# Moving three layer norms and six key transfers in the prologue of an attention and mixture-of-experts kernel

## The reference

```python
def _layernorm(x, axis=-1, eps=1e-05):
    m = jnp.mean(x, axis=axis, keepdims=True)
    v = jnp.var(x, axis=axis, keepdims=True)
    return (x - m) / jnp.sqrt(v + eps)
...
        Q = (query @ Wq.T + bq).reshape(B, Sq, H, dk).transpose(0, 2, 1, 3)
        K = (key @ Wk.T + bk).reshape(B, Sk, H, dk).transpose(0, 2, 1, 3)
        V = (value @ Wv.T + bv).reshape(B, Sk, H, dk).transpose(0, 2, 1, 3)
        scores = jnp.einsum('bhqd,bhkd->bhqk', Q, K) / jnp.sqrt(jnp.float32(dk))
        causal = jnp.tril(jnp.ones((Sq, Sk), dtype=bool))
        scores = jnp.where(causal, scores, -jnp.inf)
        attn = jax.nn.softmax(scores, axis=-1)
        out = jnp.einsum('bhqk,bhkd->bhqd', attn, V)
        out = out.transpose(0, 2, 1, 3).reshape(B, Sq, D)
        return out @ Wo.T + bo
...
    x = x + _L0_xattn_ref(_layernorm(x, axis=-1), ctx_1024, ctx_1024, ...)
    x = x + _L0_ffn_ref(_layernorm(x, axis=-1), ...)
```

## Time and profile before

| quantity | value |
|---|---|
| median of 3 timed runs | 502.96 us |
| lowest, highest | 500.89, 503.76 us |
| the profiled execution, its own time | 502.17 us |
| its span from first to last instruction | 500.3 us |
| granted TensorE clock, mean | 0.982 |
| busy: TensorE, DVE, ACT, POOL | 92%, 62%, 42%, 39% of the span |
| first projection of the loop over batches | 45.76 us after the start |

### The profile page before, as it was taken

The page is one execution under the profiler, slowest core; times in us unless marked ns, Lnnn a source line. Parts: engine busy times, 40 slices in busy tenths (PEclk is TensorE's granted clock), DMA queues, the critical chain, the costliest instruction groups (busy, mean ns, idle before and its releaser), DMA issues.

```text
span 500.3 us, 10299 instructions
## 1 busy us (share of the span) xinstructions
PE 458.4 (92%) x3154; PEld 318.9 (64%) x3155; DVE 308.2 (62%) x651; ACT 210.1 (42%) x420; POOL 193.1 (39%) x204
## 2 busy tenths in 40 slices
PE   7868999999999999988699799999999999999993
PEld 6644344654447443554256366599999999999852
DVE  4984757477563757656674796855554554555436
ACT  2254666517572566517862352523322322322210
POOL 4123545114541336201512002126666766665420
PEclk9998999999999999999979899999999999999998
DMA  8593322422124121400298900014344344444279
GB/s 263 102 229 107 108 72 65 149 65 73 64 78 145 33 95 47 138 28 2 77 371 292 367 2 21 21 33 65 64 74 74 63 71 70 70 65 74 33 197 338
DMA packets 45574, 53.84 MB, mean 108 GB/s; under 512 B 7760, under 2 KB 41872, under 8 KB 44912
## 3 DMA queue, kind: packets, MB, share of 16 engines
q1 hardware_dynamic: 34320, 39.77, 24.8%
q0 software_dynamic: 7488, 10.31, 12.8%
q10 hardware_dynamic: 3744, 3.47, 2.7%
HBM read 27.09 MB, written 13.67 MB: 81 GB/s over the span
## 4 chain that ended last, share of the span: by engine, by line
PE 68%; DVE 10%; ACT 9%; DMA 6%; issue 5%; SPq 1%; DVEq 0%; ACTq 0%; POOLq 0%
PE set_a L624 7%; PE set_b L654 7%; PE set_a L924 6%; PE set_a L925 5%; PE set_a L923 5%; ACT attention L1074 5%; PE set_a L851 5%; PE set_a L675 4%; PE set_b L644 4%; DVE attention L1306 3%; PE set_b L861 3%; PE set_b L942 3%; PE set_a L832 3%; PE set_b L943 3%; PE set_b L944 3%
## 5 line engine op out<-in xcount | busy, mean ns | idle before, releaser
L1306 DVE TENSOR_REDUCE attention<-set_a 128x2 f32<-128x1024 f32 (+2 forms) x96 | 95.9, 1042 | 28.0 <-PE set_a L626 26.1
L1074 ACT ACTIVATE attention<-set_b 128x512 f32<-128x512 f32 (+1 forms) x176 | 88.4, 570 | 58.5 <-PE set_b L644 45.8
L528 POOL TENSOR_SCALAR_AFFINE_SELECT attention<-attention 128x512 f32<-128x512 f32 x64 | 40.8, 650 | 110.4 <-ACT attention L1074 110.4
L588 POOL DMA_INDIRECT sum_rows<-moe,token_of x39 | 61.8, 1585 | 43.9 <-issue 28.9
L644 PE MATMUL set_b<-attention 99*128 99x512 bf16 (+3 forms) x256 | 60.4, 310 | 13.6 <-ACT attention L1074 10.2
L624 PE MATMUL set_a<-attention 96*128 96x512 bf16 (+3 forms) x256 | 61.5, 306 | 5.6 <-DVE attention L1306 5.4
L580 POOL DMA_INDIRECT e_x<-normed_rows,token_of x39 | 39.4, 1010 | 63.7 <-DVE token_of L1504 37.3
L1173 ACT ACTIVATE moe<-set_a 128x384 f32<-128x384 f32 x39 | 19.1, 490 | 104.9 <-PE set_a L925 104.9
L1529 DVE TENSOR_TENSOR moe<-set_a,moe 128x384 f32<-128x384 f32 x39 | 21.8, 558 | 62.7 <-ACT moe L1173 62.7
L624 PEld LDWEIGHTS set_a<-attention 96*128 96x128 bf16 x256 | 25.3, 99 | 45.3 <-DVE attention L1306 18.0
L923 PE MATMUL set_a<-wup_hi,e_xT_hi 128*128 x156 | 53.1, 340 | 0.0
(11 more groups left out here) (167 smaller groups left out, 843.5 us busy)
## 6 DMA issues: line engine op xcount, KB each, us to landing
attention<-attention SPq DMA_DIRECT2D x182, 64.0 KB, 2.6
wup<-in_wupT SPq DMA_DIRECT2D x2, 3072.0 KB, 14.6
sum_rows<-attention SPq DMA_DIRECT2D x2, 2048.0 KB, 13.6
wup<-sum_rows SPq DMA_DIRECT2D x8, 512.0 KB, 7.0
attention<-in_ctxT SPq DMA_DIRECT2D x7, 512.0 KB, 6.2
w_down<-in_wdnT SPq DMA_DIRECT2D x3, 1024.0 KB, 5.0
x_res<-in_x SPq DMA_DIRECT2D x4, 512.0 KB, 7.1
out<-x_res ACTq DMA_DIRECT2D x8, 256.0 KB, 4.0
```

The source lines that it names most:

```text
L588: g.indirect_dma_start(acc[i], bass.IndirectOffsetOnAxis(token_of[:, t:t + 1], 0), e_y[:, t % 2, :], None, compute_op=ALU.add).then_inc(ad ...
L1074: nc.scalar.activation(pT[k][:, h:h + heads, :], bank(par)[:, 0:heads * (S - k * P)], ACT.Exp).then_inc(b_free, 1)
L1306: v.tensor_reduce(dst, src, AX.X, ALU.max, negate=True).then_inc(a_free, 1)
```

## The change

- The statistics of batch 3 on DVE move from before the first split to behind the third parts of the first half.
- DVE makes one more small operation behind the moments: `st_a` becomes minus mean times 1/std for batches 1 to 3 (the shift). ACT normalises batches 1 and 2 as an activation with this bias and 1/std as scale. Batch 3 is still normalised by DVE, but behind the first maxima of group 0.
- The six key transfers of group 1 go from ACT to POOL, on a semaphore of their own, `first_keys_in`. `rows_in[1]` now counts six transfers fewer, which `rows_at` corrects in every later wait.
- TensorE makes five turns of dummy products instead of six, no longer transposes batch 1 ahead of group 0's score jobs but behind the second of them, turns the first maxima ahead of the transposes of batch 3, and makes two turns of dummy products before that instead of one. It waits for `first_keys_in` before the first slot.
- ACT waits for `first_keys_in` before it splits the second half, and copies the first maxima before the transposed batch 3.

```diff
+        def rows_at(g, units):
+
+            return DMA * (12 * units - 6 if g == 1 else 12 * units)
...
-        LN_JOB, MAX_0 = (0, 1, 2, 3), B
+        LN_JOB, MAX_0 = (0, 1, 2, 4), B - 1
...
+            def stack_keys(part):
+                pool.wait_ge((part1_ready, part2_ready, parts_ready)[part], 2)
+                for j, part_of in enumerate(K_PART):
+                    if part_of == part:
+                        g.dma_start(kstack[DK * j:DK * (j + 1), 0, HG:2 * HG, :],
+                                    parts[64:128, 1, part, :]).then_inc(first_keys_in, DMA)
+
+            for part in range(3):
+                stack_keys(part)
             pool.wait_ge(mparts_ready, 1)
             remainders(1)
...
-            keep_busy(6)
-            ln_transposes(1)
+            keep_busy(5)
             pe.wait_ge(rows_in[0], DMA * 12)
             for j in range(A_GRP):
                 rowmax_scores(0, j, 3 + j, 3 + j)
-                if j == 3:
-                    ln_transposes(2)
+                if j in (1, 3):
+                    ln_transposes(j // 2 + 1)
+            keep_busy(2)
+            maxima(MAX_0, B + 2, 1, first=True)
             ln_transposes(3)
-            keep_busy(1)
-            maxima(MAX_0, B + 2, 1, first=True)
             pe.wait_ge(fills, 3)
...
+            pe.wait_ge(first_keys_in, DMA * 6)
...
             deviations(1, QT, T)
-            for part in range(3):
-                stack_part(1, 1, part)
+
+            def normalised(b):
+
+                for j in range(QT):
+                    t = b * QT + j
+                    last = nc.scalar.activation(xs[b % 2][:, j, :], xs_all[:, t, :], ACT.Identity,
+                                                bias=st_a[:, t:t + 1], scale=rstd[:, t:t + 1])
+                last.then_inc(xs_ready, 1)
+
+            act.wait_ge(shift_ready, 1)
+            normalised(1)
+            normalised(2)
             ln_copy(1)
             nc.scalar.activation(credit[:, 2:3], ident[:, 0:1], ACT.Exp)
             ln_copy(2)
+            act.wait_ge(first_keys_in, DMA * 6)
             part1(1, 1, ((0, 1), 1))
+            max_rows(MAX_0, B + 2, 0)
             ln_copy(3)
-            max_rows(MAX_0, B + 2, 0)
             part2(1)
...
             statistics(2)
-            statistics(3)
             values(0, 0, 0)
             remainders(0)
             part3(0)
+            statistics(3)
             values(1, 1, 1)
             moments(1, QT, T, T)
+
+            v.scalar_tensor_tensor(out=st_a[:, QT:T], in0=mean[:, QT:T], scalar=-1.0, in1=rstd[:, QT:T],
+                                   op0=ALU.mult, op1=ALU.mult).then_inc(shift_ready, 1)
...
             add_v(2, 2)
-            normalised(1, lambda j: xs[1][:, j:j + 1, :]).then_inc(xs_ready, 1)
-            dve.wait_ge(b_full, LN_JOB[0] + 1)
-            normalised(2, lambda j: xs[0][:, j:j + 1, :]).then_inc(xs_ready, 1)
-            dve.wait_ge(b_full, LN_JOB[1] + 1)
-            normalised(3, lambda j: xs[1][:, j:j + 1, :]).then_inc(xs_ready, 1)
...
                 max_parts(3 + (g + 1) * A_GRP, g + 1)
+                if g == 0:
+                    dve.wait_ge(b_full, LN_JOB[2] + 1)
+                    normalised(3, lambda j: xs[1][:, j:j + 1, :]).then_inc(xs_ready, 1)
```

More of the change, by code:

```diff
@@ L251, in build @@
         st_done, ln_step, std_ready, xs_ready = sem("st_done"), sem("ln_step"), sem("std_ready"), sem("xs_ready")
-        mean_done = sem("mean_done")
+        mean_done, shift_ready = sem("mean_done"), sem("shift_ready")
         val_ready, part1_ready, rem_ready, part2_ready, parts_ready = (sem(n) for n in
@@ L257, in build @@
         rows_in = [sem(f"rows_in{g}") for g in range(NG)]
+        first_keys_in = sem("first_keys_in")
         mpart_step, mparts_ready, max_in = (sem(n) for n in
@@ L733, in slot @@
                         maxima(n_b + MAX_AT, par_b + MAX_AT, count + 2)
-            slot(0, 0, B_GRP0, B_GRP0, (3 + A_GRP, 3 + A_GRP), wait_rows=(rows_in[1], DMA * 12), order=FIRST)
+            pe.wait_ge(first_keys_in, DMA * 6)
+            slot(0, 0, B_GRP0, B_GRP0, (3 + A_GRP, 3 + A_GRP), wait_rows=(rows_in[1], rows_at(1, 1)), order=FIRST)
             pe.wait_ge(ld_ctx, DMA * (B - 1))
@@ L796, in batch @@
                 else:
-                    slot(0, count + NG, n_b, par_b, (n_a, par_a), wait_rows=(rows_in[1], DMA * 12 * (b + 2)))
+                    slot(0, count + NG, n_b, par_b, (n_a, par_a), wait_rows=(rows_in[1], rows_at(1, b + 2)))
                     n_a, par_a = n_a + A_GRP, par_a + A_GRP
@@ L1008, in part1 @@
                     for g in groups:
-                        act.wait_ge(rows_in[g], DMA * 12 * count)
+                        act.wait_ge(rows_in[g], rows_at(g, count))
                 for a in range(2):
```

## The result

The changed kernel is slower: a median of 507.88 us (four runs, 507.16 to 508.59) against 502.81 for the kernel before in the same runs, a ratio of 1.0122 with a 95% interval of 1.0091 to 1.0153. I had forecast 501.5, no measurable change, within 499.2 to 504.0.

What follows compares the result with a forecast made beforehand. TensorE, busy 92% of the span, bounds the kernel; the change touches only the prologue. Loop 1.5 us sooner: profiled 502.17 becomes 500.7, timed median 0.8 above the profiled run, so 501.5 us, range 499.2 to 504.0.

Steps and rivals of the forecast that it cites:

- The rows of group 0: Prologue, stacking transfers of queries and keys: group 0 complete at 25.0 us, bounds 23.5 and 26.5.
- I keep 7.2 us: Prologue, from the first of group 0's six reductions to the ready maxima: 7.2 us, unchanged, maxima ready at 32.8.
- DVE now does four normalisations (1.3 us): Behind the first maxima: batch 3's norm takes 1.3 us from 32.8, and group 1's score jobs start 0.7 us later.
- The clock: TensorE's clock ahead of the loop: 0.8 us gained if it falls again, 2.1 if not; mean taken, 1.5.
- my 44.3: Forecast start of the batch loop in us, its first projection, against 45.76 in the kernel before.
- Crowded engines: Rival, chance 0.20: all six POOL transfers come in front, group 0 complete at 26.5, all gain gone, 503.0 us.
- The slower case: Rival, chance 0.05: POOL needs 3.0 us per key transfer, keys land at 36.3, first scores 3.0 us late, 506.0.
- What could take it back: ACT's first copies in the loop, at 50.65, wait for SP's last key transfer; they come about 1 us sooner, nothing lost.

Runs made afterwards that it cites:

- The first experiment: The changed kernel, except that POOL's remainders of the second half wait until all four norms of batch 3 are done: ratio 1.0077 to the kernel before.

## Why the prediction was wrong

**What held.** The first split came at 13.25 (I said 13.4), SP's eighth issue at 19.24, DVE was free at 22.8 (23.1), the eight activations of ACT (0.5 us each, 4.04 in all, I took 3.2) cost nothing, and no table load was added. The shift of the loop's start reached the end: 5.5 us there, 5.1 in the medians.

**The rows of group 0** were the first failed step: 25.0 forecast, 26.3 measured, just inside the upper bound of 26.5. The rate of 2.0 transfers per us was right; the count was wrong. I took 1.0 us for an issue by POOL and it is 0.55, and I thought that about three of ACT's second six had shared the engines with group 0 in the kernel before. With the statistics alone ACT's six were issued from 21.06 on and the transfers of 19.0 to 19.6 needed 3.9 us; with POOL's keys behind group 0's rows neither these nor ACT's six stood beside them, and it was 4.0. So ACT's three had cost nothing, and POOL added six, not three: 6 / 2.0 = 3.0 us, against 7.08 - 3.9 = 3.2 measured. The stretch from 18.0 to 20.5 shows that a third queue brought no bandwidth. Changed kernel, and below it the same kernel with POOL's keys behind the rows:

```profile
18.00:20.50 2.50, 2.50 (x21) 2.18 (x20) 2.47 (x10) 0.00 (x0) 0.96 (x2) 1.00 1.12 132
```

```profile
18.00:20.50 2.50, 2.50 (x20) 2.16 (x19) 2.47 (x10) 0.00 (x0) 0.00 (x0) 1.00 0.89 177
```

The engines were busier with three queues and moved less. The Trainium skill's statement that I weighed (DMA: Bandwidth & Descriptors, "Issuing engines are not separate DMA queues") is borne out by this.

**"I keep 7.2 us"** for the reductions of group 0 was the second, by 1.2 us. The wait for the rows had become 4.04 us of idle TensorE, and the jobs behind it ran at the lower clock (0.59 on average); with the clock kept up by dummies the stretch took 7.34. I had worked out that DVE would be idle for 2.5 us there and did not ask what the same wait does to TensorE.

**"DVE now does four normalisations (1.3 us)"** was the third and the one I had no bound for: 3.08. I looked for what POOL does beside the norms only among its transfers. But POOL's remainders and the moved norm are released by the same event, the parts of the first maxima, so the change puts them side by side. Before, the norms ran while POOL waited for these parts. The Trainium skill has the rule (SBUF — State Buffer, "SBUF: two separate sides"): VectorE in a mode that uses both of its ports and GpSimd exclude each other for a whole instruction. I cited the section for descriptors and passed over its main sentence. The first experiment agrees that the two get in each other's way: 1.37 us without POOL beside it. That they exclude each other for a whole instruction no row here shows. By the same page POOL's six issues could have been slow; here they were not (0.55 us each).

**The clock** was the fourth and the dearest. I let it decide between 0.8 and 2.1 us of gain in a stretch of 3.4 us. The transposes of batch 3 took 1.97 instead of 1.09 us, and the jobs behind them ran at half speed for 8.8 us. The idle stretches ahead of this were 1.39 and 2.61 us; for the second I had expected 1.0, the rest being the slow norms. Dummies in them kept the clock up. But the length of the idle stretch alone does not decide. With POOL's remainders behind the norms it was 0.91 and the jobs ran slow again; with POOL's keys from 21.2 on it was 1.74 and they did not:

```profile
39.00:47.50 8.50, 7.90 (x40) 4.09 (x38) 6.21 (x7) 4.73 (x9) 3.75 (x5) 0.60 0.24 79
```

```profile
35.40:44.30 8.90, 7.08 (x54) 3.58 (x52) 6.90 (x10) 6.89 (x13) 3.60 (x5) 1.00 0.39 105
```

What decides stays open. At full clock the job series is bound by the reductions and the loop comes 3.6 us sooner, as the dummies showed.

In sum, from my 44.3 to 51.28: +1.3 to 1.5 rows, +1.2 first jobs at half clock, +2.6 norms and transposes (1.7 and 0.9), +1.8 for the jobs of group 1. That is 7.0. Of the 1.8 half stands ahead of the first scores: 3.4 us from group 1's first job (40.30 to 43.72) where I had 2.5, as the clock was low from the first job on and not only from the first scores on as in the earlier trace rows. The other half stands behind them: 7.56 us where I had 6.7, the mean of a slow and a fast case, and the slow one came (7.39 before).

**The rivals.** "Crowded engines" had nearly the right landing, 26.5, and the wrong price, since it took no clock and no port with it. The slower case had a wrong mechanism: the keys by POOL were through before 25, and nothing waited for them.

**A step that the changed kernel could not test** failed too. "What could take it back" let ACT's first copies in the loop come about 1 us sooner with the loop. In the four versions whose loop began 1.4 to 2.7 us sooner than before they still stood at 50.31 to 50.68, waiting for SP's transfers.

**What the parts are worth.** Moving only POOL's issues by 6 us takes the changed kernel from 1.0122 to 0.9996: crowding is the root of most of the loss, since the long waits and, with them, much of the clock's share come from it. The same crowding without the rest of the change costs 0.2%, so its price depends on what waits behind it. The slowed norms are worth 1.7 us by themselves. The statistics are a gain of 0.4%, through a transfer that I had treated as a constant of 3.87 us and through the clock behind it. The norms on ACT never ran without the rest.

## What to carry to other kernels

When a transfer is moved to an idle queue, ask what it overtakes: six transfers that nobody needed for 10 us delayed the ones that everybody waited for by 3 us, on engines that were already full. When an operation is moved behind an event, list what else that event releases, on the engine with which it shares ports above all. And price each new wait twice, once for the engine that waits and once for the clock of TensorE behind it. And run the parts of a change alone: here the smallest one, four statistics moved, was faster than the whole and than the kernel before.

## What the runs showed of the hardware

- A plain transfer of 64 KB issued by POOL occupies it for 0.55 us (six in 3.32), less than the 0.65 of SP's, and needed 4.1 us in the median to land among the others. The DMA table of the changed kernel, 0 to 50 us, counts 192 packets for POOL's six, 32 each; ACT's queue has 480 fewer over the whole kernel (3264 instead of 3744) with six transfers fewer, 80 each:

```profile
q0 software_dynamic: 192, 0.39, 5.3%
```

- A DMA share above 1 with fewer GB/s: 0.89 and 177 GB/s with two queues, 1.12 and 132 GB/s with three in the same 2.5 us.
- A transfer of 12 KB took effect 3.87 us after its copy began beside the end of a bulk load, and 2.96 us when the load was through.
- Four VectorE operations of 128x256 took 3.08 us beside POOL's subtraction and 1.37 alone, while POOL's pair took 2.31 instead of 2.27.
